# Encoder of a language-model tower: the products with the values move one group later, and the two dense units of a group stand together

## The reference

```
for l in range(L):                                   # L = 4 layers
    y = _layer_norm(h, ln_a[l, 0], ln_b[l, 0])
    qkv = jnp.einsum('bsd,tde->tbse', y, attn_w[l, :3]) + attn_b[l, :3][:, None, None, :]
    q, k, v = [t.reshape(b, s, H, DK).transpose(0, 2, 1, 3) for t in qkv]   # H = 16, DK = 16
    scores = jnp.einsum('bhqd,bhkd->bhqk', q, k) * inv_sqrt_dk
    p = jax.nn.softmax(scores, axis=-1)
    o = jnp.einsum('bhqk,bhkd->bhqd', p, v).transpose(0, 2, 1, 3).reshape(b, s, D)
    h = h + o @ attn_w[l, 3] + attn_b[l, 3]
    y = _layer_norm(h, ln_a[l, 1], ln_b[l, 1])
    h = h + jax.nn.relu(y @ w1[l] + b1[l]) @ w2[l] + b2[l]
```

## Time and profile before

| | us |
|---|---|
| median of 3 runs | 2148.15 (2146.69 to 2149.09) |
| the profiled execution: its time | 2149.03 |
| the profiled execution: its span | 2147.2 |
| encoder, from the start to PE's first matmul of the next stage | 1315.7 |
| one full slot (slot 14, from its first scores to those of slot 15) | 38.88 |

### The profile page before, as it was taken

The page is one execution under the profiler, slowest core; times in us unless marked ns, Lnnn a source line. Parts: engine busy times, 40 slices in busy tenths (PEclk is TensorE's granted clock), DMA queues, the critical chain, the costliest instruction groups (busy, mean ns, idle before and its releaser), DMA issues. The chain is left out here.

```text
span 2147.2 us, 42189 instructions
## 1 busy us (share of the span) xinstructions
PE 2056.3 (96%) x16462; PEld 1663.5 (77%) x16462; DVE 1299.4 (61%) x3344; ACT 1033.1 (48%) x3525; POOL 215.7 (10%) x249
## 2 busy tenths in 40 slices
PE   5899999999999999999999998999999999699997
PEld 3688888888888888888888876787777788577775
DVE  4676776766767667667677744677766465122222
ACT  3656566666565665656666643454545421011110
POOL 4000000000000000000000000000000000513443
PEclk9999999999999999999999999999999999799999
DMA  5000000100000300000000004000001000124441
GB/s 178 1 1 2 2 1 2 68 1 2 2 2 2 152 2 1 2 2 2 2 2 1 2 1 162 18 1 1 1 1 47 13 11 10 47 79 151 147 141 41
DMA packets 27203, 69.84 MB, mean 33 GB/s; under 512 B 9920, under 2 KB 17825, under 8 KB 23680
## 3 DMA queue, kind: packets, MB, share of 16 engines
q1 hardware_dynamic: 18432, 59.42, 8.2%
q0 software_dynamic: 6400, 5.63, 1.0%
q10 hardware_dynamic: 2176, 2.10, 0.3%
HBM read 61.16 MB, written 17.40 MB: 37 GB/s over the span
## 5 line engine op out<-in xcount | busy, mean ns | idle before, releaser
L547 ACT ACTIVATE probs<-bank,nmax 128x256 f32<-128x256 f32 x1024 | 475.1, 479 | 413.1 <-DVE nmax L716 413.1
L716 DVE TENSOR_REDUCE nmax<-bank 128x2 f32<-128x512 f32 x512 | 318.1, 683 | 209.4 <-PE bank L401 209.3
L414 PE MATMUL bank<-ident,probs 128*128 128x128 f32 x2048 | 271.9, 276 | 5.1 <-DVE pts L724 5.1
L414 PEld LDWEIGHTS bank<-ident,probs 128*128 128x128 f32 x2048 | 232.7, 141 | 39.8 <-DVE pts L724 22.7
L446 PE MATMUL bank<-yT,weights 128*128 128x256 f32 x1024 | 249.4, 387 | 0.9 <-ACT aT L570 0.9
L458 PE MATMUL bank<-weights,aT 128*128 128x256 f32 x1024 | 232.6, 380 | 1.3 <-DVE h L754 0.8
L547 ACT ACTIVATION_READ_ACCUMULATOR probs<-bank,nmax 128x1 f32 x1024 | 215.9, 211 | 0.0
L446 PEld LDWEIGHTS bank<-yT,weights 128*128 128x128 f32 x1024 | 185.3, 191 | 38.2 <-ACT aT L570 11.6
L458 PEld LDWEIGHTS bank<-weights,aT 128*128 128x128 f32 x1024 | 189.5, 190 | 25.3 <-DVE h L754 1.2
L724 DVE COPY pts<-bank 128x512 f32<-128x512 f32 x256 | 173.2, 677 | 38.3 <-PE bank L414 38.3
L556 ACT ACTIVATE pts<-bank 128x512 f32<-128x512 f32 x256 | 156.9, 613 | 20.5 <-PE bank L414 17.6
(11 more groups left out here) (217 smaller groups left out, 2941.4 us busy)
## 6 DMA issues: line engine op xcount, KB each, us to landing
wqkv<-in_experts SPq DMA_DIRECT2D x16, 1024.0 KB
weights<-in_wtok SPq DMA_DIRECT2D x4, 2048.0 KB, 19.1
wqkv<-in_experts SPq DMA_DIRECT2D x16, 512.0 KB
expert_rows<-xT_all SPq DMA_DIRECT2D x10, 546.0 KB, 16.5
xrows<-expert_rows SPq DMA_DIRECT2D x16, 273.0 KB, 2.9
weights<-in_wtok SPq DMA_DIRECT2D x3, 1024.0 KB
wqkv<-in_wqkv SPq DMA_DIRECT2D x1, 3072.0 KB, 18.0
weights<-in_shared SPq DMA_DIRECT2D x1, 3072.0 KB, 10.9
```

Source lines behind the costliest of these rows:

```text
L414: last = pe.transpose(g[:, (NT * x + kb) * P:(NT * x + kb + 1) * P], p[:, x, kb * P:(kb + 1) * P], ident[:])
L547: last = nc.scalar.activation(probs[u % 8][:, x, :], g[:, x * S:(x + 1) * S], ACT.Exp, bias=nmax[j % 2][:, col:col + 1], accum_out=rsum[j ...
L716: nc.vector.tensor_reduce(nmax[j % 2][:, col:col + 2], g[:].rearrange("p (x s) -> p x s", x=2), AX.X, ALU.max, negate=True).then_inc(s_max, 1)
```

## The change

The list of what stands where, for a group c of slot j (small transposition in brackets):

- PE before: scores, first dense unit, turn 0 and 1, [small transposition, or in c3 `ffn_up` 2], turn 2 and 3, second dense unit, `pv` of the group before; in c2 `ffn_up` 0 behind that.
- PE after: scores, `pv` of the group before the last, turn 0 and 1, both dense units (in c0 and c1 the `ffn_down` that was last; in c2 `y2_T` behind q and k), turn 2 and 3, then r_T, y_T, `ffn_up` 0 or `ffn_up` 3.

ACT does the four `exps` of a group in a row and its other work before or behind them. DVE does `fed_forward` within the group, `normalise(2, ..)` and `o_norm` between the second and third `row_max`, and `bias(j-1, R_BO)` at the end of c0. The second dense unit and the small transpositions use other banks. What is computed is the same.

```
@@ the bank of each use @@
+                jq, cq = divmod(GROUPS * j + c - 2, GROUPS)
+                if cq == 0:
+                    use((jq, "o"), 6)
+                for n in range(4):
+                    use((jp, "pt", 4 * cp + n), 4 + n % 2)
                 if c == 0:
-                    use((j, "v"), 7), use((j - 1, "rT"), 0), use((j - 2, "down", 0), 7)
+                    use((j, "v"), 7), use((j - 2, "down", 0), 0), use((j - 1, "rT"), 7)
                 if c == 1:
-                    use((j - 1, "wo"), 7), use((j + 1, "yT"), 0), use((j - 2, "down", 1), 7)
+                    use((j - 2, "down", 1), 0), use((j - 1, "wo"), 1), use((j + 1, "yT"), 7)
                 if c == 2:
-                    use((j + 1, "q"), 7), use((j - 1, "y2T"), 0), use((j + 1, "k"), 1), use((j - 1, "up", 0), 7)
+                    use((j + 1, "q"), 7), use((j + 1, "k"), 1), use((j - 1, "y2T"), 0), use((j - 1, "up", 0), 7)
...
@@ PE @@
                     scores(j, c)
+                    pv(jq, cq)
+                    turn_probs(jp, cp, 0)
+                    turn_probs(jp, cp, 1)
...
                     if c == 0:
                         values(j)
+                        ffn_down(j - 2, 0)
                     if c == 1:
+                        ffn_down(j - 2, 1)
                         project_out(j - 1)
                     if c == 2:
                         feature_major(j + 1, "q", 0)
+                        feature_major(j + 1, "k", 1)
+                        y2_T(j - 1)
                     if c == 3:
                         ffn_up(j - 1, 1)
-                    turn_probs(jp, cp, 0)
-                    turn_probs(jp, cp, 1)
+                        ffn_up(j - 1, 2)
+                    turn_probs(jp, cp, 2)
+                    turn_probs(jp, cp, 3)
                     if c == 0:
                         r_T(j - 1)
                     if c == 1:
                         y_T(j + 1)
...
-                    if c < 2:
-                        ffn_down(j - 2, c)
-                    if c == 2:
-                        feature_major(j + 1, "k", 1)
-                    if c == 3:
-                        ffn_up(j - 1, 3)
-                    pv(jp, cp)
...
                     if c == 2:
                         ffn_up(j - 1, 0)
+                    if c == 3:
+                        ffn_up(j - 1, 3)
@@ ACT @@
-                    exps(j, c, 0)
-                    exps(j, c, 1)
+                    if c == 1:
+                        r_out(j - 1)
+                    if c == 2:
+                        y_out(j + 1, "yT", 0)
+                    if c == 3:
+                        relu(j - 1, 0)
+                    for n in range(4):
+                        exps(j, c, n)
                     copy_pt(jp, cp, 1)
...
                     if c == 2:
                         y_out(j - 1, "y2T", 1)
-                        copy_pt(jp, cp, 3)
...
+                        k_out(j + 1)
                     if c == 3:
                         relu(j - 1, 2)
...
+                    copy_pt(jp, cp, 3)
@@ DVE @@
+                    row_max(j, c, 0)
+                    row_max(j, c, 1)
                     if c == 1:
-                        fed_forward(j - 2, 0)
                         o_norm(j - 1)
                     if c == 2:
-                        fed_forward(j - 2, 1)
-                    row_max(j, c, 0)
-                    row_max(j, c, 1)
+                        normalise(2, j - 1)
                     row_max(j, c, 2)
                     row_max(j, c, 3)
                     copy_pt(jp, cp, 0)
@@ -809,7 +803,9 @@
                         v_out(j)
                         if j > 0:
                             stats_of(1, j + 1)
+                        fed_forward(j - 2, 0)
                     if c == 1:
+                        fed_forward(j - 2, 1)
                         attended(j - 1)
                         stats_of(2, j - 1)
...
                     if c == 0:
                         normalise(1, j + 1)
-                    if c == 1:
-                        normalise(2, j - 1)
+                        bias(j - 1, R_BO)
```

More of the change, by code:

```diff
@@ L199, in embed_and_encoder @@
                     use((j, "S", 4 * c + n), n)
+                jp, cp = divmod(GROUPS * j + c - 1, GROUPS)
+                jq, cq = divmod(GROUPS * j + c - 2, GROUPS)
[3 more added lines that the diff above has]
+                    use((jp, "pt", 4 * cp + n), 4 + n % 2)
                 if c == 0:
-                    use((j, "v"), 7), use((j - 1, "rT"), 0), use((j - 2, "down", 0), 7)
+                    use((j, "v"), 7), use((j - 2, "down", 0), 0), use((j - 1, "rT"), 7)
                 if c == 1:
-                    use((j - 1, "wo"), 7), use((j + 1, "yT"), 0), use((j - 2, "down", 1), 7)
+                    use((j - 2, "down", 1), 0), use((j - 1, "wo"), 1), use((j + 1, "yT"), 7)
                 if c == 2:
-                    use((j + 1, "q"), 7), use((j - 1, "y2T"), 0), use((j + 1, "k"), 1), use((j - 1, "up", 0), 7)
+                    use((j + 1, "q"), 7), use((j + 1, "k"), 1), use((j - 1, "y2T"), 0), use((j - 1, "up", 0), 7)
                 if c == 3:
                     use((j - 1, "up", 1), 7), use((j - 1, "up", 2), 0), use((j - 1, "up", 3), 7)
[L208 to L212, removed]
                 for n, u in enumerate(SECOND.get((j, c), ())):
@@ L486, in _ @@
                     jp, cp = divmod(GROUPS * j + c - 1, GROUPS)
+                    jq, cq = divmod(GROUPS * j + c - 2, GROUPS)
                     scores(j, c)
+                    pv(jq, cq)
+                    turn_probs(jp, cp, 0)
+                    turn_probs(jp, cp, 1)
+                    if (j, c) == (JOBS + 1, 0):
+                        for u in SECOND[j, c]:
+                            second(u)
                     if c == 0:
                         values(j)
+                        ffn_down(j - 2, 0)
                     if c == 1:
+                        ffn_down(j - 2, 1)
                         project_out(j - 1)
@@ L501, in _ @@
                         y_T(j + 1)
-                    if c == 2:
-                        y2_T(j - 1)
-                    if c == 3:
[L505 to L510, removed]
-                    if c < 2:
-                        ffn_down(j - 2, c)
-                    if c == 2:
-                        feature_major(j + 1, "k", 1)
-                    if c == 3:
-                        ffn_up(j - 1, 3)
-                    pv(jp, cp)
                     if (j, c) != (JOBS + 1, 0):
@@ L604, in _ @@
                     jp, cp = divmod(GROUPS * j + c - 1, GROUPS)
-                    exps(j, c, 0)
-                    exps(j, c, 1)
-                    copy_pt(jp, cp, 1)
-                    exps(j, c, 2)
-                    if c == 0:
-                        r_out(j - 1)
-                    if c == 1:
-                        y_out(j + 1, "yT", 0)
+                    if c == 1:
[6 more added lines that the diff above has]
+                        exps(j, c, n)
+                    copy_pt(jp, cp, 1)
                     if c == 2:
                         y_out(j - 1, "y2T", 1)
-                        copy_pt(jp, cp, 3)
-                    exps(j, c, 3)
+                        k_out(j + 1)
                     if c == 3:
                         relu(j - 1, 2)
[L619 to L622, removed]
+                    copy_pt(jp, cp, 3)
                     for u in SECOND.get((j, c), ()):
                         second_out(u)
-                    if c == 2:
-                        relu(j - 1, 0)
         @block.vector
@@ L752, in attended @@
                     return
+                step.wait(dve)
                 g = take(dve, (j, "wo"))
@@ L755, in attended @@
                 evacuated(dve, (j, "wo"))
-                bias(j, R_BO)
             def fed_forward(j, i):
@@ L821, in _ @@
                         normalise(1, j + 1)
-                    if c == 1:
-                        normalise(2, j - 1)
+                        bias(j - 1, R_BO)
                     if c == 2:
+                        if real(j - 1):
+                            dve.wait_ge(s_yn[1], j)
                         bias(j - 1, R_B2)
```

## The result

The changed kernel takes 2153.27 us as the median of 9 runs (2150.70 to 2158.86), the kernel before 2147.08 beside it (9 runs, 2143.67 to 2150.81): a ratio of 1.0033, with a 95% interval of 1.0024 to 1.0043. It is 6 us slower, where 4.6 us less were forecast (2143.5 against 2148.15). Its span is 2157.1 us, 9.9 above that of before; 2.1 of these lie behind the encoder, in code that is the same (833.6 against 831.5 us), and are no effect of the change. The next stage starts at 1323.47 instead of 1315.7 us; these 7.8 us are the subject.

The account below looks back on a forecast made before the run. PE's own stream was taken to bound a full slot. Full slots +0.3, `second_norm` +2.5, start -7.0 and end -0.6 sum to -4.8 on the profiled 2149.0, itself 0.9 above the median: 2143.5 us; forecast 2139 to 2148, range 2125 to 2156.

Parts of the forecast that it names:

- The late row maximum of c1: DVE, late from c0, starts it 1.53 us into c1; `ffn_down` then waits for bank 0, 0.31 lost plus 0.10.
- `y_out`'s wait in c2: In c2 `ffn_up` 0 waits for ACT's `y_out` behind `y2_T`: 0.42 us lost plus 0.10 for the new start.
- the end: Slot 31 to the next stage: shorter c0, c1 and c2, a later last `pv`; -0.6 us in all.
- `second_norm`: Extra DVE work in slots 28 to 30 that delays PE: 4.1 us after against 1.6 today, so +2.5 us.
- The start: Slots 0 and 1: `pv` no longer waits for its own group's last copy; slot 2 starts earlier, -7.0 us.
- The allowance of 1.5 us for a low clock: Slots 0 and 1: one more low-clock stretch doubles some 1.5 us of work, making 8.5 us earlier into -7.0.
- Scores ahead of `pv`: PE's price for scores followed by `pv`, in every group: taken as 1.07 us, the other bound being 0.94.
- The step that failed: New PE waits in a full slot: `ffn_down` in c1 (0.31 plus 0.10 us), `ffn_up` 0 in c2 (0.42 plus 0.10).
- "No wait any more of the transpositions for DVE's copies": A sign expected in the profile after: in full slots PE's transpositions no longer wait for DVE's copies.
- The slower one (DVE's chain across c0): Rival: copy, `normalise` and `bias` after `fed_forward` delay c1's row maximum, 2.9 us per 0.1; 2153 to 2162, chance 0.2.
- The clock in slots 0 and 1: Rival: the clock stays low there and groups take today's time; -1 to +1, 2147 to 2150 us, chance 0.15.
- The faster one: Rival: scores ahead of `pv` cost 0.94 (11 us), without the two waits 27; 2117 to 2133 us, chance 0.2.

Follow-up runs that it names:

- the first experiment: The changed kernel with DVE copying the third transposition out ahead of the layer-norm statistics in c1; 2142.78 us, ratio 0.9977 to the kernel before.
- all three edits: The changed kernel with the copy ahead of the statistics in c1, bias ahead of `fed_forward` in c0, and `y2_T` between q and k; 2115.51 us, ratio 0.9849.
- the dose: Also the fifth experiment: the changed kernel with `bias(j - 1, R_BO)` between `attended` and the statistics in c1, no longer at c0's end; 2166.16 us, one run.
- second: The changed kernel with DVE doing `bias(j - 1, R_BO)` ahead of `fed_forward` in c0; 2137.52 us, one run.
- third: The changed kernel with PE doing `y2_T` between q and k in c2 instead of behind k; 2140.99 us, one run.

## Why the prediction was wrong

*The frame held.* A full slot is PE's stream plus its waits: the groups without an unforeseen wait came out within 0.03 us, and so did the seams (`ffn_up` 0 lost the one towards `pv`; the scores still follow it). The late row maximum of c1 is there as worked out. DVE and PE's weight loads in order of time, end of c0 and c1 of slot 14 of the changed kernel:

```profile
573.67 0.42 DVE L758 TENSOR_TENSOR h<-h,bank 128x256 f32<-128x256 f32 x1 [1.61 <-PE bank L459]
...
575.83 0.68 DVE L742 TENSOR_TENSOR h<-h,rows 128x512 f32<-128x512 f32 x1
576.43 1.28 DVE L711 TENSOR_REDUCE nmax<-bank 128x2 f32<-128x512 f32 x2
...
578.22 3.32 PEld L459 LDWEIGHTS bank<-weights,aT 128*128 128x128 f32 x16 [0.41 <-ACT probs L547]
```

It starts 1.55 behind the scores (574.88), forecast 1.53, and the first load of `ffn_down` 1.79 later, as forecast. `y_out`'s wait in c2 is there too. In the sum, the end comes out as forecast and `second_norm` within 0.5 us.

*The start is right in part by luck.* Its sum was off by 0.1 us, its pieces by more. Two of its groups, as stretches of the changed kernel (columns as in the earlier trace rows), c2 of slot 0 and c1 of slot 1:

```profile
40.22:48.38 8.16, 8.06 (x82) 6.71 (x81) 5.49 (x10) 6.16 (x22) 1.28 (x1) 0.93 0.02 9
63.29:73.61 10.32, 8.03 (x77) 6.35 (x77) 7.11 (x19) 5.32 (x20) 0.72 (x1) 0.83 0.01 2
```

The first was taken as 10.2 with 2.3 us at half the clock and measured 8.16 at a mean clock of 0.93; the second was taken as 8.1 and measured 10.32 at 0.83, and c0 of slot 1 took 8.15 instead of 7.2. The allowance of 1.5 us for a low clock happened to make up the difference. The sum's -4.8 from 2148.15 is also 2143.35 and not 2143.5, and a row maximum at 1.7 would have taken the whole forecast gain of 4.8, not the start's 7.0; nothing rests on either.

*Scores ahead of `pv`* cost 1.08 (565.27 to 566.35), and not the lower bound of 0.94. PE's weight loads in order of time, c0 of slot 14 of the changed kernel:

```profile
566.35 0.81 PEld L431 LDWEIGHTS bank<-pts,v 128*32 128x32 f32 x32 [0.33 <-issue]
567.36 0.86 PEld L415 LDWEIGHTS bank<-ident,probs 128*128 128x128 f32 x8 [0.20 <-issue]
568.18 1.60 PEld L376 LDWEIGHTS bank<-weights,yT 128*128 128x128 f32 x8
569.80 3.43 PEld L459 LDWEIGHTS bank<-weights,aT 128*128 128x128 f32 x16
```

The loads of `pv` halt for 0.33 us behind those of the scores. What the Trainium skill, page "TensorE: Matmul & The Clock Gate", section "The mechanism", says, that a weight load overlaps matmuls in flight only where its row group differs, gave the right price for this pair. As a general rule the trace does not bear it out: the loads of `values` and `ffn_down` (568.18 and 569.80) use all rows, as do the matmuls in flight, and run on without a halt. In these slots the halts that no wait explains stand where the shape of the tiles changes.

*The step that failed* is the list of new waits. It named `ffn_down` in c1 and `ffn_up` 0 in c2, and left out `pv` in c2. The prediction gave `pv` its 1.01 in each group and never asked for its inputs' time. Its own way of counting would have found the wait, though only just: from its start of `ffn_down` at 3.42, with 3.46 for it, 1.89 for `project_out`, and, as in the kernel before, about 0.7 for `attended`, 0.95 for the statistics and 0.66 for the copy, my estimate has the copy end 1.1 us behind the scores of c2, where `pv` is due at 1.07; measured it is 1.24. Measured in place of no wait: 0.42 us in c2 (10.53 against 10.10 to 10.11 with only that order changed), 12.2 us over 29 slots. That is more than the whole difference between the forecast 2143.5 and the measured 2153.3; the first experiment, without that wait, has 2142.8.

*"No wait any more of the transpositions for DVE's copies"* was right as far as it goes, and hid the point: the wait for the same copy moved on to the next reader.

*The rivals.* The slower one (DVE's chain across c0) named the right engine and the right price, 2.9 us for each 0.1 us of lateness, but the wrong place: that chain came out as forecast, and the one through `project_out` and the statistics in c1 did it. That its 2153 to 2162 hold the measured time is a coincidence. The clock in slots 0 and 1 did not stop the gain. The faster one had both its assumptions wrong: scores ahead of `pv` pay the full seam, and both forecast waits are there.

*The chances.* Slower had 0.22, faster 0.47. The measured time lies within the range of 2125 to 2156, but outside the forecast's 2139 to 2148, and the full slot of 39.33 is further from 38.9 than the 0.15 that the prediction allowed. A sum within 0.2% of no change, in which two chains already reach PE and each 0.1 us more costs 2.9 us, gave no ground for twice as much on faster.

## What to carry to other kernels

When a product is moved later than its inputs' making, list each reader's inputs anew with the time of the last one, on the engine that makes it; the wait that disappears in front of one reader can reappear in front of the next. On an engine with strict order, what another engine waits for in a fixed place of the loop (a copy out of a bank, a row maximum) goes ahead of what nobody awaits soon (statistics, bias): two such moves, and one on PE that asks earlier for what ACT needs long for, each of one or two lines, turned a loss of 0.3% into a gain of 1.5%. Try the halves of a change apart: the later `pv` gained 0.5% by itself, and the other half paid only when all three of its waits were gone (with one gone the kernels took 2137.5 to 2142.8, against 2134.4 for `pv` alone). Price the pieces of an in-order loop from start to start, not by their busy times; with seams counted, the sum for a slot without waits was 37.96 and the kernel with all three edits took 38.03.

## What was not expected of the hardware

From the end of DVE's copy to the first weight load of the waiting `pv` 0.22 us pass (586.15 to 586.37 in the changed kernel, 589.37 to 589.59 in the dose), while a transposition that waits for such a copy starts its load 0.05 behind it (c0 of slot 14 of the kernel before, 570.90 to 570.95). The difference of 0.17 is part of the 0.42 us. Why, no run here tells; between the two, the tile shape and the work ahead on PE differ.

How slots 0 and 1 fall out differs from execution to execution of like kernels: slot 2 starts at 90.25, 90.64, 92.42 and 92.03 us in the first, second, third and fifth experiment, and at 93.27 in the changed kernel, with the same work there but for one or two pieces. So the start's 6.9 us is good to some 3 us. Why, no run here tells.
